# A four-block transformer kernel on one core: the experts' input is turned once per mixture and reloaded by transposing DMAs

## What is computed

```python
shared = silu(xt @ sg_w.T) * (xt @ su_w.T) @ sd_w.T        # inner width 512 (second mixture: 384)
topk_p, topk_idx = top_k(sigmoid(xt @ router_w.T + bias), 2)   # 8 experts; second: softmax, no bias
g = einsum('th,eih->tei', xt, wg); u = einsum('th,eih->tei', xt, wu)
y = einsum('tei,ehi->teh', silu(g) * u, wd)                # inner width 512 (second: 192)
out = shared + einsum('te,teh->th', w, y)                  # w: the two chosen weights
```

## Time and profile before

| | |
|---|---|
| median of three runs | 2046.61 us (2046.53 to 2051.81) |
| profiled execution | 2046.28 us, its span 2044.1 us |
| busy share of the span | PE 82%, PEld 47%, DVE 72%, ACT 54%, POOL 20% |
| mean granted TensorE clock | 0.904 of full |
| router and route, first / second mixture | from 255.9 to 308.3 us / from 1635 to 1686 us |
| shared expert, first / second | 308.3 to 450 us / 1686 to 1814 us |
| routed experts, first / second | 451 to 783 us / 1815 to 1976 us |
| DMA | 164.09 MB in 113033 packets, 80 GB/s on average |

### The profile page before, as it was taken

The page is one execution under the profiler, slowest core; times in us unless marked ns, Lnnn a source line. Parts: engine busy times, 40 slices in busy tenths (PEclk is TensorE's granted clock), DMA queues, the critical chain, the costliest instruction groups (busy, mean ns, idle before and its releaser), DMA issues. The chain is left out here.

```text
span 2044.1 us, 43859 instructions
## 1 busy us (share of the span) xinstructions
PE 1667.6 (82%) x15250; PEld 953.9 (47%) x15250; DVE 1477.2 (72%) x2895; ACT 1098.1 (54%) x2248; POOL 418.3 (20%) x533
## 2 busy tenths in 40 slices
PE   2897259999999993767999999999997358889950
PEld 1775148976666662321222222222225247767740
DVE  4776677764444446869999999999936776656657
ACT  1443415643333332534999999999993415444422
POOL 2000206631222222220000000000000206534432
PEclk9998759999999996776999999999998759999985
DMA  5600004541111113332121111120005003323445
GB/s 200 276 0 6 31 1 153 157 125 48 60 58 61 58 53 127 119 94 54 37 60 48 47 47 45 48 60 24 17 17 175 24 1 110 113 87 120 126 148 174
DMA packets 113033, 164.09 MB, mean 80 GB/s; under 512 B 20246, under 2 KB 89756, under 8 KB 110556
## 3 DMA queue, kind: packets, MB, share of 16 engines
q1 hardware_dynamic: 97340, 117.85, 19.1%
q0 software_dynamic: 15520, 43.93, 5.9%
HBM read 89.07 MB, written 72.37 MB: 79 GB/s over the span
## 5 line engine op out<-in xcount | busy, mean ns | idle before, releaser
L1499 DVE TENSOR_REDUCE sa_row_max<-psum 128x1 f32<-128x1024 f32 x512 | 582.5, 1217 | 12.3 <-PE psum L1381 12.2
L1482 ACT ACTIVATE sa_probs<-psum 128x512 f32<-128x512 f32 x1024 | 549.6, 597 | 37.8 <-PE psum L1432 28.3
L1381 PE MATMUL psum<-v_k_max,v_q_stack 48*128 48x512 f16 x1024 | 301.4, 398 | 24.4 <-DVE sa_row_max L1499 16.2
L1412 PE MATMUL psum<-sa_probs,sa_v_now 128*32 128x256 f32 (+1 forms) x3840 | 321.0, 406 | 0.1
L1432 PE MATMUL psum<-v_q_stack,sa_k_main 49*128 49x512 f16 x1024 | 309.8, 384 | 2.0 <-ACT sa_probs L1482 1.2
L1993 PE MATMUL psum<-m0w_all,m0fx_xt_high 128*128 x568 | 193.4, 382 | 0.6 <-DVE m0fx_xt_low L1925 0.6
L1432 PEld LDWEIGHTS psum<-v_q_stack,sa_k_main 49*128 49x128 f16 x1024 | 64.6, 94 | 222.3 <-ACT sa_probs L1482 208.5
L1412 PEld LDWEIGHTS psum<-sa_probs,sa_v_now 128*32 128x32 f32 x3840 | 75.7, 108 | 189.9 <-issue 100.1
L1939 DVE TENSOR_TENSOR m0fx_ht_low<-psum,m0fx_ht_high 128x512 f16<-128x512 f32 x71 | 49.1, 692 | 134.4 <-ACT m0fx_ht_high L1907 134.4
L1901 ACT ACTIVATE m0fx_gate<-psum 128x512 f32<-128x512 f32 x71 | 42.4, 598 | 152.7 <-PE psum L1993 148.4
L1884 POOL DMA_INDIRECT y_rows<-m0fx_y_sb,m0fx_x_in x71 | 68.3, 962 | 274.1 <-DVE m0fx_y_sb L1946 274.1
(11 more groups left out here) (371 smaller groups left out, 3737.6 us busy)
## 6 DMA issues: line engine op xcount, KB each, us to landing
x_rows<-la_blank SPq DMA_DIRECT2D x18, 1032.0 KB, 8.2
v_q_stack<-q_scratch SPq DMA_DIRECT2D x192, 64.0 KB, 2.4
m0fx_x_in<-x_rows SPq DMA_DIRECT2D x71, 129.0 KB, 2.0
m1fx_x_in<-x_rows SPq DMA_DIRECT2D x71, 129.0 KB
m0fs_stage<-in_up SPq DMA_DIRECT2D x16, 512.0 KB
m0g_got<-y_rows SPq DMA_DIRECT2D x32, 256.0 KB, 3.8
o_scratch<-sa_o_sb POOLq DMA_DIRECT2D x32, 256.0 KB, 2.5
wo_o_in<-o_scratch SPq DMA_DIRECT2D x32, 256.0 KB, 3.6
```

The source lines that it names most:

```text
L1381: nc.tensor.matmul(mx_ps[m % 2][:, half * 512:(half + 1) * 512], q_stack[h][side:side + ROWS, head, qt * P:(qt + 1) * P], k_max[side:side ...
L1412: last = nc.tensor.matmul(o_ps[32 * g:32 * g + 32, cols], v_now[:, kt, kv, :], probs[(GROUPS * step + g) % 16][:, cols], start=(kt == 0), ...
L1482: nc.scalar.activation(probs[at % 16][:, :], st_ps[bank_of(at)][:, :], ACT.Exp, scale=0.25 / (QK_SCALE * QK_SCALE)).then_inc(s["expd"], 1)
L1499: nc.vector.tensor_reduce(row_max[n % 2][:, at % QT, column:column + 1], mx_ps[m % 2][:, :], AX.X, ALU.max).then_inc(s["maxed"], 1)
```

## The change

x is turned once per mixture, in `router_logits`. The two fp16 parts of all 32 turned tiles stay in SBUF, in the memory of `core.y` (`core.xt`; the shared expert reads tile i there before it writes `core.y` of tile i). The shared expert takes them from there. Its row buffers no longer hold x as 256 floats but as 256 high and 256 low fp16 values in the same bytes, the same for both choices; ACT and DVE now make these parts from the unturned x, for both copies in one instruction each of 2 x 256 elements. The routed experts no longer turn x on PE: SP loads each tile by four transposing DMAs of 128 x 128 fp16 values (two parts, two halves of the columns) and one DMA of the two tail values. The loops of `router_logits` and of the shared expert become straight code. Bias, maxima and index searches move from `route` into `router_logits`, for a quarter of the tiles at a time, a step per group. Cut to its core:

```diff
 class Core:
+        self.xt = self.y[:, :, :].bitcast(F16).rearrange("p t (a k q) -> p t a k q", a=2, k=KD)
 def shared_expert
+        xhat = [ph.sb(f"xhat{j}", [P, D]) for j in range(UNROLL)]
+        x_parts = [x_in[j][:, :, :].bitcast(F16) for j in range(UNROLL)]
-            for k in range(PEELED):
-                turn(k)
-            with eng.Fori(PEELED, TURNS - PEELED) as k:
-                turn(k)
-            for k in range(TURNS - PEELED, TURNS):
+            for k in range(TURNS):
                 turn(k)
 ...
-                    pool.wait_ge(s["x_ready"], i + 1)
+                    pool.wait_ge(s["x_low"], i + 1)
                     for c in range(2):
-                        if c == 1:
-                            pool.wait_ge(s["x_again"], i + 1)
 ...
+                def x_high(i, w, k):
                     j = w % UNROLL
                     act.wait_ge(s["x_ready"], i + 1)
                     ge(act, sent[j], (k + w // UNROLL) * 32)
-                    nc.scalar.activation(x_in[j][:, 1, 0:D], x_in[j][:, 0, 0:D], ACT.Copy).then_inc(s["x_again"], 1)
+                    nc.scalar.activation(x_parts[j][:, :, 0:D], xhat[j][:, :].unsqueeze(1).to_broadcast([P, 2, D]),
+                                         ACT.Copy).then_inc(s["x_high"], 1)
 ...
+                def x_low(i, w, k):
+                    j = w % UNROLL
+                    dve.wait_ge(s["x_high"], i + 1)
+                    ge(dve, sent[j], (k + w // UNROLL) * 32)
+                    nc.vector.tensor_tensor(x_parts[j][:, :, D:2 * D], xhat[j][:, :].unsqueeze(1).to_broadcast([P, 2, D]),
+                                            x_parts[j][:, :, 0:D], ALU.subtract).then_inc(s["x_low"], 1)
 ...
-                    if real(i + 2):
-                        low(i + 2, j)
+                    if real(i + 1):
+                        x_low(i + 1, u + 1, k)
 ...
-                        pe.wait_ge(s["xt_low"], i + 1)
-                        up(gate_ps[j], j, F).then_inc(s["gated"], 1)
+                        up(gate_ps[j], i, F).then_inc(s["gated"], 1)
-                    if real(i + 2):
-                        turn(i + 2, j, u + 2)
 def routed_experts
+    LOADS = 16 * 2 * KD
-        x_in = [ph.sb(f"x_in{j}", [P, ROW]) for j in range(ROWS_HELD)]
+        x_tail = [ph.sb(f"x_tail{j}", [P, ROW - D]) for j in range(ROWS_HELD)]
+        xt = [ph.sb(f"xt{j}", [P, 2, KD, P], F16) for j in range(ROWS_HELD)]
 ...
-                    sp.dma_start(x_in[i % ROWS_HELD][:, :], x_rows[i, :, :]).then_inc(x_loaded[i % ROWS_HELD], 16)
+                    for a in range(2):
+                        for k in range(KD):
+                            at = a * D + k * P
+                            sp.dma_start(xt[i % ROWS_HELD][:, a, k, :], x_rows[i, :, :].bitcast(F16)[:, at:at + P],
+                                         transpose=True).then_inc(x_loaded[i % ROWS_HELD], 16)
+                    sp.dma_start(x_tail[i % ROWS_HELD][:, :], x_rows[i, :, D:ROW])\
+                        .then_inc(tail_loaded[i % ROWS_HELD], 16)
 ...
-                    pe.wait_ge(s["xt_low"], i + 1)
+                    pe.wait_ge(x_loaded[i % ROWS_HELD], (i // ROWS_HELD + 1) * LOADS)
 ...
-                    if i + 2 < n:
-                        turn(i + 2, j)
 def router_logits
+    ROUND = 4
+    xt = core.xt
 ...
+                norm(0)
+                for g in range(NG):
+                    if g + 1 < NG:
+                        norm(g + 1)
+                    low(g)
+                    q, at = divmod(g - ROUND - 1, ROUND)
+                    if q >= 0:
+                        (keep, maxima, find)[at](q) if at < 3 else None
+                keep(NG // ROUND - 1)
+                maxima(NG // ROUND - 1)
+                find(NG // ROUND - 1)
```

More of the change, by code:

```diff
@@ L2136, in _ @@
                 dve.wait_ge(masks, 6)
-                if bias_row is not None:
-                    dve.wait_ge(bias_in, 16)
-                    then(nc.vector.tensor_tensor(r.logits[:, :, :], r.logits[:, :, :],
-                                                 bias[:, :].unsqueeze(1).to_broadcast([P, T, E]), ALU.add))
-                for t in range(T):
-                    last = nc.vector.max(top[:, t, :], r.logits[:, t, :])
-                then(last)
-                for t in range(T):
-                    last = nc.vector.max_index(index[:, t, :], top[:, t, :], r.logits[:, t, :])
-                then(last)
                 then(nc.vector.tensor_copy(index_f[:, :, :], index[:, :, 0:2]))
@@ L2211, in _, with router_logits @@
                                                     in1=pairs[:, :, 0], op0=ALU.mult, op1=ALU.add))
-def router_logits(core, name, router, logits):
+def router_logits(core, name, router, bias_row, top, index):
     nc = core.nc
@@ L2219, in router_logits, with turned, part, _ @@
     NG = T // G
+    ROUND = 4
+    xt = core.xt
     with Phase(nc, name) as ph:
+        bias = ph.sb("bias", [P, E])
         xhat = [ph.sb(f"xhat{j}", [P, G, D]) for j in range(2)]
-        xt = [[ph.sb(f"xt_{x}{j}", [P, G * KD, P], F16) for x in ("high", "low")] for j in range(2)]
+        logits = ph.sb("logits", [P, T, E])
         turn_ps = [ph.ps() for j in range(2)]
-        logit_ps = ph.ps()
-        s = {n: ph.sem(n) for n in ("xhat_done", "turned", "high", "low", "logged", "kept")}
+        logit_ps = [ph.ps() for j in range(2)]
+        s = {n: ph.sem(n) for n in ("bias_in", "xhat_done", "turned", "high", "low", "logged", "kept", "maxed", "found")}
+        def turned(j):
+            return turn_ps[j][:, :].rearrange("p (u t) -> p u t", u=G)
+        def part(g, a):
+            return xt[:, g * G:(g + 1) * G, a, :, :].rearrange("p u k t -> p u (k t)")
         with ph.block() as block:
+            @block.sync
+            def _(sp):
+                if bias_row is not None:
+                    sp.dma_start(bias[:, :], bias_row.to_broadcast([P, E])).then_inc(s["bias_in"], 16)
             @block.tensor
             def _(pe):
-                def turn(g, j):
+                def turn(g):
                     pe.wait_ge(s["xhat_done"], g * G + G)
@@ L2264, in _ @@
             @block.scalar
             def _(act):
-                def high(g, j):
+                for g in range(NG):
                     act.wait_ge(s["turned"], g + 1)
-                    ge(act, s["logged"], g - 1)
-                    nc.scalar.activation(xt[j][0][:, :, :], turn_ps[j][:, :].rearrange("p (k t) -> p k t", t=P),
-                                         ACT.Copy).then_inc(s["high"], 1)
-                tiles(act, NG, 2, high)
+                    nc.scalar.activation(part(g, 0), turned(g % 2), ACT.Copy).then_inc(s["high"], 1)
@@ new lines, in maxima, with find @@
+                def maxima(q):
+                    dve.wait_ge(s["kept"], q + 1)
+                    for t in tiles_of(q):
+                        last = nc.vector.max(top[:, t, :], logits[:, t, :])
+                    last.then_inc(s["maxed"], 1)
+                def find(q):
+                    dve.wait_ge(s["maxed"], q + 1)
+                    for t in tiles_of(q):
+                        last = nc.vector.max_index(index[:, t, :], top[:, t, :], logits[:, t, :])
+                    last.then_inc(s["found"], 1)
@@ L2308, in mixture @@
+                norm(0)
+                for g in range(NG):
+                    if g + 1 < NG:
+                        norm(g + 1)
[6 more added lines that the diff above has]
+                find(NG // ROUND - 1)
+                dve.wait_ge(s["found"], NG // ROUND)
 @contextmanager
@@ L2322, in mixture @@
                                    router[1][:, :, :])])
-                    router_logits(core, name + "rl", router, r.logits)
-                    route(core, name + "r", r, normalise, bias_row)
+                    top = pl.sb("top", [P, T, 8])
+                    index = pl.sb("index", [P, T, 8], mybir.dt.uint32)
+                    router_logits(core, name + "rl", router, bias_row, top, index)
+                    route(core, name + "r", r, normalise, top, index)
                 shared_expert(core, name + "fs", w_shared, x_rows, r, w, (up_r, down_r), filled)
```

183 lines of the change are left out of this document (53 added, 130 removed).

## The result

The changed kernel takes 2366.74 us (median of four runs, 2359.70 to 2370.90), the kernel before beside it 2049.17 us (four runs, 2046.53 to 2051.81): a ratio of 1.155 (95% interval 1.152 to 1.158), 317 us more where I forecast 21. The profiled execution took 2359.7 us with a span of 2357.7, 313.6 more than before.

What follows compares the result with a forecast made beforehand. PE was taken to bound the routed experts and the first shared expert. From 2046.3 us, -5 (router, route), -17 (shared), -15.6 (routed PE) and +59 (load queue) gave +21, so 2068 us; 8-in-10 range 2020 to 2370.

Steps and rivals of the forecast that it cites:

- the price of one transposing issue: Routed experts' SP queue: 0.617 us per transposing load, 2.95 us per tile; hidden in first mixture, +59 us in second.
- Rival B: Routed experts: transposes hardly overlap in the DMA engines, 5.28 us per tile, +57 and +224 us, 2306 us total; chance 0.33.
- The two rules: Skill passages on DMA transposes: as fast as regular DMAs (2028 us), or 1309 ns per 128x128 transpose (2368 us).
- Router and route: Moved bias, maxima and searches: gains 6.4 and 4.6 us, less 2.9 per mixture in the router; sum -5 us.
- Shared experts: Dropped PE transposes save 7 and 6 us, earlier starts 3.8; sum -17 us, bounds -26 and -5.
- Routed experts, PE: Dropping a pair of transposes saves PE 0.22 us per tile, -15.6 us in the first mixture.
- The first tile changes nothing: Start of routed experts: four loads awaited instead of one, but no turn, high and low part follow; no change.
- The clock: Routed experts, second mixture: idle PE may fall to 1.2 GHz, costing up to 60 us; taken as 0.

## Why the prediction was wrong

**The step that failed is the price of one transposing issue.** I took 0.617 us from a plain load in 256-byte pieces; it is 1.232. Put into my own sum: 4 x 1.232 + 0.577 = 5.5 us per tile, (5.5 - 4.47) x 71 = +73 and (5.5 - 2.12) x 71 = +240; the measured paces, with the gaps between issues, give +87 and +243. The form of the step held (SP's queue never waits for the stores, issues without pause, PE waits for xt), only it also took the first mixture, which I had let PE's 4.25 us cover. The measured 2367 us lies inside the range for 8 times in 10, but only just, and by a rival's mechanism; the forecast's own range ended at 2120.

**The choice between the ends was the fault.** A transposing load had no row in the trace, the bounds were 0.445 and 2.0 us, and I chose by the size of its pieces. The run with plain loads shows that this likeness was worth little: the same pieces without a turn take 0.432 us, less than the row I took, and the turn adds 0.8. Here the turn set the price, not the pieces.

**Rival B had the size right by luck and the place wrong.** Its 1.2 us per load came from the movement of a plain load, put into the DMA engines, and gave 5.28 us per tile and 2306 us. But the DMA engines' share is 0.20, they deliver the same bytes in 2.04 us per tile once the instructions are fewer, and an issue costs 1.18 us after SP has been idle for 14.6. The pace is set where the loads are issued. This changes what helps: if B's mechanism were right, no grouping of tiles would have gained anything. One number of B is off too: at 0.94 us per load SP only begins to bind the first mixture; slower than before it gets from (4.47 - 0.477) / 4 = 1.0.

**The two rules.** The Trainium skill, VectorE: DVE Perf Modes, section The three transpose paths, gives 1309 ns for a 128x128 transpose by DMA; the runs show 1232 per issue, and the estimate worked out from it, 5.71 us per tile and 2368 us, fits the measured 5.71, 5.59 and 2367 (in part by chance: a lower price, but a dearer tail and gaps). But read as a price per 128x128 block the figure fails: 512 rows take 1.262 us, not four times that. The Trainium skill, Advanced Engine Details and Errata, section X-Bar Transpose (TRN2), says that transposes are as fast as regular DMAs: per instruction they are not (1.232 against 0.432), while the bytes kept up with PE's 2.04 us per tile in the run with four tiles.

**Router and route:** predicted gains 6.4 and 4.6, cost of the moved searches 2.9 each. From the last transpose of the router to the experts of the tiles it is 19.3 and 19.0 us after, 25.7 and 23.7 before: 6.4 and 4.7, as worked out. The stretch of the transposes grew by 1.9 and 1.7 us (27.1 from 25.2 and 25.4). -7.5 in all, -5 predicted. DVE's timeline answers to the earlier trace rows: the last of the index searches, and 2.2 us behind it the cast, once POOL's mask is there.

```profile
291.13 0.16 DVE L2246 FIND_INDEX8 m0l_index<-m0l_top,m0rl_logits 128x8 uint32<-128x8 f32 x1
293.34 0.20 DVE L2073 CAST m0r_index_f<-m0l_index 128x64 f32<-128x64 uint32 x1 [2.05 <-POOL m0r_before L2046]
```

**Shared experts:** predicted -17, measured -28.6 (8.8 and 19.8) in the changed kernel's profile, but the same code gives between -17.3 (two transposes per tile) and -28.7 (64 rows) in the other profiles. The paces (against the earlier trace rows, hidden values):

```profile
L1734 DVE SCALAR_TENSOR_TENSOR m0fs_hidden<-psum,m0fs_gate x32: 678/684/694, 312.4 to 435.8; 128x512 f32<-128x512 f32 x32
...
L1734 DVE SCALAR_TENSOR_TENSOR m1fs_hidden<-psum,m1fs_gate x32: 545/551/558, 1770.2 to 1870.5; 128x384 f32<-128x384 f32 x32
```

(435.8 - 312.4) / 31 = 3.98 us, predicted 3.99; (1870.5 - 1770.2) / 31 = 3.24, predicted 3.6, while I had written 3.31 as PE's own need. With two transposes per tile the same code ran at 3.50:

```profile
L1734 DVE SCALAR_TENSOR_TENSOR m1fs_hidden<-psum,m1fs_gate x32: 541/551/558, 1663.3 to 1771.7; 128x384 f32<-128x384 f32 x32
```

So the forecast of 3.6 lies near the slow end of what this code shows, and the surplus of 11.6 us over the predicted 17 is within the spread. What varies are the waits of the earlier trace rows: "issue" 9.0 us before, 3.5 after, 5.7 with two transposes per tile; DVE's low parts 4.0, 1.8 and 5.6. DVE's wider low part (681 ns, I had allowed 740) binds nothing. The version with float32 rows, at 139.5 and 122.9 us, lies beyond the spread in both stages (by 1.4 and 4.5 us), so the rows made in a buffer of their own seem to help; why one kernel's stage is faster than another's with the same code stays open.

**Routed experts, PE:** the 0.22 us per tile of the earlier trace rows is confirmed where PE binds: 4.26 us in the first mixture with plain loads or with groups, 4.25 predicted, and with groups of four tiles the stage gains 11.6 us of the 15.6 after a later start. "The first tile changes nothing" was wrong: the first result comes 5 and 11 us later than before, since it waits for the loads of three tiles, 12 transposing issues and more.

**The clock:** I took no fall. In the second routed stage it is 0.65 on average, between the two levels, with PE busy 236 of 415 us, and a product that took 326 ns at the median in the run with four tiles takes 527. That it costs nothing there, as PE waits for SP in any case, is argued; no run separates it.

## What to carry to other kernels

Before loads are replaced by transposing ones, count the instructions per step of the loop, and multiply by what one holds the issuing queue (here 1.23 us, against 0.43 for a plain one): that product is a pace of its own, beside those of the engines, and the busy share of the DMA engines (0.20 here) does not show it. When an operation has no row in the trace, the nearest row by size is no price for it; give the gap between the bounds its weight, and look for the design whose result doesn't hang on it. Here that was one instruction for four tiles, which turned 15% slower into 2.3% faster than before.

## What the runs showed of the hardware

- A transposing DMA issue takes 1.228 us for 64 rows of 128 two-byte values and 1.300 for 1024 rows; a straight line through the two leaves some 1.22 that don't depend on the rows, an estimate. The shortest, such as the one behind a tail's load, take 1.09.
- The price doesn't come from transposes that are still under way: after 14.6 us without an issue a load of 1024 rows took 1.18 us, and the first of the stage, 128 rows at 440.46, took 1.20.
- A plain load of 256-byte pieces takes 0.432 us on SP's queue, and so does the load of the tails between such loads; between transposing ones the tails' load takes 0.577. Why was not tested.
- The landing time of a transposing load of 128 rows is 2.4 us, only 0.4 above the plain load's 2.0 in the earlier trace rows, though its issue takes 0.9 longer than that load's.
- The same straight code of the second shared expert took from 110.0 to 118.4 us in seven kernels that differ only in the routed experts. A difference of some us between one profile of one kernel and one of another is no effect of the code by itself.
